# A two-layer transformer kernel: the first feed-forward's residual, and the transposition and absorption of the second layer's weights, as one stage

## Time and profile before

| what | us |
|---|---|
| median of three runs | 3326.28 |
| the profiled execution's own time | 3329.78 |
| its span, first to last instruction | 3328.0 |
| f0r, from its first load | 1346.54 to 1382.10 |
| w1t | 1382.10 to 1425.73 |
| w1u, and the start of w1a | 1425.73 to 1452.12 |
| w1a from its first store | 1452.12 to 1497.60 |
| l1n0 | 1497.60 to 1523.35 |
| l1p0 | 1523.35 to 1601.86 |

### The profile page before, as it was taken

One profiled execution on the slowest core, in us unless ns is written; L12 is line 12 of the kernel. 1 busy time (PEld: TensorE's weight loads), 2 busy tenths in 40 slices (PEclk: granted clock), 3 DMA queues, 4 the chain that ended last, 5 costly groups with the idle time before them and its releaser, 6 DMA issues. The chain is left out here.

```text
span 3328.0 us, 42805 instructions
## 1 busy us (share of the span) xinstructions
PE 2881.2 (87%) x14636; PEld 2302.2 (69%) x14636; DVE 1909.6 (57%) x3654; ACT 1189.4 (36%) x2311; POOL 998.4 (30%) x784
## 2 busy tenths in 40 slices
PE   7969999769999999257799999957999999399994
PEld 6846666547777777237688888746888888288883
DVE  5648877464344444435466666654666666644445
ACT  2226666422222211113244444322444444233331
POOL 1227777534454546303100000033000000222223
PEclk9969999879999999678899999978999999699997
DMA  5764443222111101662000000040000000300002
GB/s 175 232 207 130 133 128 110 68 92 73 46 55 43 57 26 37 217 275 105 28 32 24 23 32 22 18 155 28 23 26 29 22 33 18 125 15 20 19 1 101
DMA packets 137219, 249.58 MB, mean 75 GB/s; under 512 B 14368, under 2 KB 78880, under 8 KB 136320
## 3 DMA queue, kind: packets, MB, share of 16 engines
q1 hardware_dynamic: 137088, 247.91, 22.8%
HBM read 168.43 MB, written 79.17 MB: 74 GB/s over the span
## 5 line engine op out<-in xcount | busy, mean ns | idle before, releaser
L1067 POOL TENSOR_TENSOR l0a_probs_hl<-l0a_probs,l0a_probs_hl 128x896 fp32r<-128x896 f32 (+1 forms) x128 | 284.9, 2245 | 107.1 <-ACT l0a_probs L995 107.1
L1299 PE MATMUL l1a_obank<-l1a_pT_hl,l1k_v_hl 128*128 128x512 f32 (+3 forms) x1152 | 300.7, 370 | 7.2 <-DVE l1a_pT_hl L1372 7.1
L1325 ACT ACTIVATE l1a_probs<-l1a_scores,l1a_row 128x128 f32<-128x128 f32 (+7 forms) x256 | 189.5, 742 | 318.1 <-DVE l1a_row L1362 318.1
L1372 DVE TENSOR_TENSOR l1a_pT_hl<-l1a_work,l1a_pT_hl 128x512 fp32r<-128x512 f32 (+3 forms) x384 | 212.9, 554 | 155.0 <-ACT l1a_pT_hl L1332 154.8
L1415 POOL TENSOR_TENSOR l1a_q_stage<-l1k_qpe,l1a_ones 128x512 fp32r<-128x512 f32 x32 | 33.3, 1041 | 877.0 <-PE l1a_work L1307 820.3
L1279 PE MATMUL l1a_scores<-l1k_kT_hl,l1a_qa_hl 128*128 128x512 f32 (+3 forms) x1152 | 291.9, 362 | 1.5 <-ACT l1a_probs L1325 1.5
L1629 PE MATMUL f0f_ybank<-f0f_wT,f0f_h_hl 128*128 128x512 f32 x768 | 203.5, 417 | 35.4 <-POOL f0f_h_hl L1745 35.3
L1332 ACT CAST l1a_pT_hl<-l1a_work 128x512 fp32r<-128x512 f32 (+3 forms) x384 | 183.7, 478 | 107.6 <-PE l1a_work L1290 106.4
L1307 PE MATMUL l1a_work<-l1a_wov,l1a_oT_hl 128*128 128x512 f32 x768 | 215.2, 403 | 5.0 <-DVE l1a_oT_hl L1391 3.0
L1362 DVE TENSOR_REDUCE l1a_row<-l1a_scores 128x1 f32<-128x128 f32 (+7 forms) x256 | 189.7, 750 | 45.0 <-PE l1a_scores L1282 44.9
L1386 DVE SCALAR_TENSOR_TENSOR l_acc<-l1a_work,l1a_row,l_acc 128x512 f32<-128x512 f32 x256 | 189.4, 750 | 35.5 <-PE l1a_work L1307 27.1
(11 more groups left out here) (253 smaller groups left out, 6202.6 us busy)
## 6 DMA issues: line engine op xcount, KB each, us to landing
v_dram<-l0f_v_rows SPq DMA_DIRECT2D x24, 768.0 KB, 4.2
qk_dram<-l0f_stage SPq DMA_DIRECT2D x128, 128.0 KB, 2.5
l1a_wov<-wov_dram SPq DMA_DIRECT2D x32, 512.0 KB, 3.4
l0a_v_stage<-v_dram SPq DMA_DIRECT2D x32, 384.0 KB, 4.2
l1a_wabs<-wabs_dram SPq DMA_DIRECT2D x32, 384.0 KB, 3.8
l0a_q_stack<-qk_dram SPq DMA_DIRECT2D x32, 256.0 KB, 3.5
l0a_k_stack<-qk_dram SPq DMA_DIRECT2D x32, 256.0 KB, 3.8
f0f_chunk<-in_L_ffn_w_gate_up SPq DMA_DIRECT2D x32, 256.0 KB, 2.8
```

The costliest lines, as they stand in the source:

```text
L1067: nc.gpsimd.tensor_tensor(probs_hl[:, r, 1, 0:wide], probs[:, r, 0:wide], f32(probs_hl[:, r, 0, 0:wide]), ALU.subtract).then_inc(low_done, 1)
L1299: last = pe.matmul(obank[:, c:SPAN], src["v_hl"][:, a, n, :], pT_hl[:, ring(n, s), b, c:SPAN], start=(n == 0 and i == 0), stop=(n == QT * ...
L1325: nc.scalar.activation(probs[s][:, first:first + wide, :].rearrange("p k c -> p (k c)"), scores[:, n % S_AHEAD, 0:wide * P], ACT.Exp, bias ...
L1372: nc.vector.tensor_tensor(pT_hl[:, r, 1, c:SPAN], work[:, slot, c:SPAN], f32(pT_hl[:, r, 0, c:SPAN]), ALU.subtract).then_inc(work_free[slo ...
```

## The change

One function, `residual_and_weights`, replaces the stages f0r, w1t, w1u and w1a; the `clear_semaphores` between f0r and w1t goes.

- VectorE runs the first 6 row steps (LEAD), then alternates: low half of job n, row step 6 + n; then the last row step, then the low halves of the 16 heads. Within a row step bn_aggr is moved behind z of two tiles earlier. ScalarE runs 6 roots, then alternates the copy of job n and root 6 + n. GpSimd adds as before.
- owT shrinks from 16 heads to a ring of 4, filled two heads ahead within the head loop: TensorE turns o_w of head h + 2 before the products of head h, ScalarE copies it (before: VectorE). o_w and q_nope are loaded in four pieces of four heads each, in SyncE's order below.
- wabs and wov get semaphores of their own: ScalarE waits for the store of wabs (h - 2) and of wov (h - 2) separately, SyncE stores wabs as soon as it is ready.
- waT and wpT are allocated outside (right side of the memory, where xT0 was, which is given up at that point) and stay on chip until l1p of batch 0 is over. Their stores to DRAM, for batch 1, move into l1p0, issued by SyncE at its start. l1n0 no longer loads them; l1n1 does.

```diff
-                with phase("f0r") as m:
-                    residual(nc, m, NT, x1, x2, lambda t: acc[:, t, :])
-        clear_semaphores()
-        with phase("w1") as w:
...
+                hold.close()
+                wk = kept.enter_context(phase("wk"))
+                waT = wk.sb("waT", [P, 2, KT, QL + LAT + ROPE], F32R, side="right")
+                wpT = wk.sb("wpT", [P, 2, 3, NH * ROPE], F32R, side="right")
+                with phase("w1") as m:
...
+                    residual_and_weights(nc, m, ident, x1, x2, acc, sources, waT, wpT, wabs_dram, wov_dram)
         clear_semaphores()
...
+def residual_and_weights(nc, m, ident, src, dst, acc, w, waT, wpT, wabs_dram, wov_dram):
+    RING, LAG, HEADS, AHEAD, LEAD = 4, 2, 4, 2, 6
+    ow = m.sb("ow", [P, 2, KT, HEADS * P])
+    owT = m.sb("owT", [P, RING, D])
...
+        @block.sync
+        def _(sp):
+            def load_rows(g):
+                wait(sp, sum_done, QT * (g - 1))
+                sp.dma_start(x[:, g % 2 * QT:(g % 2 + 1) * QT, :],
+                             src[g * SPAN:(g + 1) * SPAN, :].rearrange("(t p) d -> p t d", p=P)).then_inc(x_loaded[g % 2], 16)
+            def store_rows(g):
+                for t in range(g * QT, (g + 1) * QT):
+                    sp.wait_ge(sum_done, t + 1)
+                    sp.dma_start(dst[t * P:(t + 1) * P, :], z[:, t % RING, :]).then_inc(x_stored[t % RING], 16)
+            def load_ow(i):
+                wait(sp, turned, J + HEADS * (i - 1) if i >= 2 else 0)
+                sp.dma_start(ow[:, i % 2], w["ow"][:, :, i * HEADS * P:(i + 1) * HEADS * P]).then_inc(ow_loaded[i], 16)
+            def store_head(h):
+                sp.wait_ge(a_low, h + 1)
+                sp.dma_start(wabs_dram[h], f32(wabs[:, h % 2])).then_inc(a_stored[h % 2], 16)
+                sp.wait_ge(v_low, h + 1)
+                sp.dma_start(wov_dram[h], f32(wov[:, h % 2])).then_inc(v_stored[h % 2], 16)
+            sp.dma_start(qa[:, :, :], w["qa"]).then_inc(down_loaded, 16)
+            sp.dma_start(kva[:, 0, :], w["kva"][0]).then_inc(down_loaded, 16)
+            sp.dma_start(kva[0:ROPE, 1, :], w["kva"][1]).then_inc(down_loaded, 16)
+            load_rows(0)
+            for e in range(2):
+                sp.dma_start(qp[e * ROPE:(e + 1) * ROPE], w["qp"][e]).then_inc(pe_loaded, 16)
+            load_rows(1)
+            load_q(0)
+            load_ow(0)
+            store_rows(0)
+            load_rows(2)
+            sp.dma_start(k_b[:, :, :], w["k_b"]).then_inc(kb_loaded, 16)
+            store_rows(1)
+            load_rows(3)
+            sp.dma_start(v_b[:, :, :], w["v_b"]).then_inc(vb_loaded, 16)
+            load_q(1)
+            load_ow(1)
+            store_rows(2)
+            store_rows(3)
+            load_q(2)
+            for h in range(NH):
+                store_head(h)
+                if h == 1:
+                    load_ow(2)
+                    load_q(3)
+                if h == 5:
+                    load_ow(3)
...
+        @block.tensor
...
+            for h in range(AHEAD):
+                turn(h)
             for h in range(NH):
-                wait(pe, low, 2 * (h - 1))
+                if h + AHEAD < NH:
+                    turn(h + AHEAD)
+                if h % HEADS == 0:
+                    pe.wait_ge(q_loaded[h // HEADS], 16)
+                wait(pe, a_low, h - 1)
                 for j in range(3):
                     last = pe.matmul(abank[:, h % 2, j * P:(j + 1) * P], q_nope[:, h, j * P:(j + 1) * P],
                                      k_b[:, h, :], start=True, stop=True)
+                last.then_inc(a_full, 1)
+                pe.wait_ge(ow_copied, h + 1)
+                wait(pe, v_low, h - 1)
+                pe.matmul(vbank[:, h % 2, :], v_b[:, h, :], owT[:, h % RING, :], start=True, stop=True
+                          ).then_inc(v_full, 1)
         @block.scalar
...
+            for t in range(LEAD):
+                root(t)
+            for n, (blocks, view, hi, lo) in enumerate(jobs):
+                act.wait_ge(turned, n + 1)
+                nc.scalar.copy(hi, view(bank[:, n % RING])).then_inc(job_high, 1)
+                if LEAD + n < NT:
+                    root(LEAD + n)
+            for h in range(AHEAD):
+                copy_ow(h)
             for h in range(NH):
+                act.wait_ge(a_full, h + 1)
+                wait(act, a_stored[h % 2], 16 * (h // 2))
...
+                if h + AHEAD < NH:
+                    copy_ow(h + AHEAD)
+                act.wait_ge(v_full, h + 1)
+                wait(act, v_stored[h % 2], 16 * (h // 2))
...
         @block.vector
+            def row(t):
+                if t < NT:
+                    r = t % RING
+                    nc.vector.bn_stats(stats[:, r, :], acc[:, t, :]).then_inc(stats_done, 1)
+                if t >= LAG:
+                    u = t - LAG
+                    r = u % RING
+                    dve.wait_ge(std_done, u + 1)
+                    nc.vector.reciprocal(rstd[:, r:r + 1], std[:, r:r + 1]).then_inc(rstd_done, 1)
+                    dve.wait_ge(rstd_done, u + 1)
+                    wait(dve, x_stored[r], 16 * (u // RING))
+                    nc.vector.tensor_scalar(z[:, r, :], acc[:, u, :], mv[:, r, 0:1], rstd[:, r:r + 1],
+                                            ALU.subtract, ALU.mult).then_inc(z_done, 1)
+                if t < NT:
+                    r = t % RING
+                    dve.wait_ge(stats_done, t + 1)
+                    nc.vector.bn_aggr(mv[:, r, :], stats[:, r, :]).then_inc(mv_done, 1)
+            for t in range(LEAD):
+                row(t)
+            for n, (blocks, view, hi, lo) in enumerate(jobs):
+                dve.wait_ge(job_high, n + 1)
+                nc.vector.tensor_tensor(lo, view(bank[:, n % RING]), f32(hi), ALU.subtract).then_inc(job_low, 1)
+                if LEAD + n < NT + LAG:
+                    row(LEAD + n)
+            for t in range(LEAD + J, NT + LAG):
+                row(t)
...
-def latent_operands(nc, m, ident, xT_hl, waT, wpT, norm_w, rope, out):
+def latent_operands(nc, m, ident, xT_hl, waT, wpT, norm_w, rope, out, stores=()):
+        @block.sync
+        def _(sp):
+            for dst, tile in stores:
+                sp.dma_start(dst, tile).then_inc(stored, 16)
+            wait(sp, stored, 16 * len(stores))
```

More of the change, by code:

```diff
@@ L1805, in absorbed_weights @@
     wabs = m.sb("wabs", [P, 2, 2, 3, LAT], F32R)
     wov = m.sb("wov", [P, 2, 2, D], F32R)
[L1807 to L1810, removed]
-    with nc.Block() as block:
+    bank = m.ps("bank", [P, RING, SPAN])
+    abank, vbank = m.ps("abank", [P, 2, SPAN]), m.ps("vbank", [P, 2, SPAN])
+    jobs = [([(qa[:, i, c * P:(c + 1) * P], i * P) for i in range(3)] + [(kva[:, 0, c * P:(c + 1) * P], 3 * P)],
+             bank_part(SPAN), waT[:, 0, c, 0:SPAN], waT[:, 1, c, 0:SPAN]) for c in range(KT)]
@@ new lines, in residual_and_weights @@
+    jobs.append(([(kva[0:ROPE, 1, c * P:(c + 1) * P], c * ROPE) for c in range(KT)], bank_part(KT * ROPE, KT),
+                 waT[:, 0, :, SPAN:SPAN + ROPE], waT[:, 1, :, SPAN:SPAN + ROPE]))
+    jobs += [([(qp[:, 4 * g + i, j * P:(j + 1) * P], i * P) for i in range(4)], bank_part(SPAN),
+              wpT[:, 0, j, g * SPAN:(g + 1) * SPAN], wpT[:, 1, j, g * SPAN:(g + 1) * SPAN])
+             for j in range(3) for g in range(2)]
+    J = len(jobs)
+    x_loaded = [m.sem(f"x_loaded{i}") for i in range(2)]
@@ L1835, in _ @@
         @block.vector
         def _(dve):
-            for h in range(NH):
[L1838 to L1845, removed]
-                par = h % 2
-                sp.wait_ge(low, 2 * h + 2)
-                sp.dma_start(wabs_dram[h], f32(wabs[:, par])).then_inc(stored[par], 16)
-                sp.dma_start(wov_dram[h], f32(wov[:, par])).then_inc(stored[par], 16)
-            for par in range(2):
-                sp.wait_ge(stored[par], 32 * NH // 2)
@@ L2168, in two_layers @@
                         with phase(f"l1p{b}") as m:
-                            latent_operands(nc, m, ident, xT, waT, wpT, norm_w, (cos, sin), ops)
+                            latent_operands(nc, m, ident, xT, waT, wpT, norm_w, (cos, sin), ops,
+                                            kept_pairs if b == 0 else [])
+                    kept.close()
                     with phase(f"l1a{b}") as m:
```

151 lines of the change are left out of this document (102 added, 49 removed).

## The result

The changed kernel takes 3284.05 us (median of 4 runs, 3277.77 to 3286.7) against 3326.52 for the kernel before on the same chip: ratio 0.9873, 95% interval 0.9851 to 0.9894, that is 42.5 us less (interval 35 to 50). The prediction said 3285. One execution of e1_keep_only (3652 us) and one of the kernel before (7911 us) were in a slow state of the chip, and the ratios of the experiments leave them out.

What follows compares the result with a forecast made beforehand. DMA engines were taken as the common resource of a serial seam with four kinds of waits. Seam 61.3 + 52 = 113.3 against 151.1 us, 37.8 less, plus 3.3 in the next stage: 41.1 less, median 3285, range 3268 to 3303.

Steps and rivals of the forecast that it cites:

- Steps 1 to 3: Seam from first load through residual rows and weight jobs: first absorbed store at 61.3 us.
- row 0 behind the queued loads: Residual rows: row 0's store moves behind the first queued weight loads, landing at about 25 us, and z(4) waits for it.
- the ring of two engines: Residual rows with jobs: VectorE and ScalarE wait on each other in turn, 3.1 us a row.
- a second queueing at z(12): Residual rows: store 8 lands behind later loads at 51.3 us, so z(12), ready at 49.8, waits.
- Step 4: Head loop: 52 us, the middle between 49.3 (all bytes at 397 GB/s) and 55.4 (no added load absorbed).
- the finer wait: Head loop: ScalarE's first half of a head waits for its own store only, giving back up to 0.2 us a head.
- Step 5: Norm stage of batch 0: without the waT and wpT loads the following stage starts 3.3 us sooner (0 to 4.2).
- Step 6: Batch 0's latent_operands: the moved waT and wpT stores, 5.5 MB taking 32 us, cost nothing there.
- A: Rival for the seam: stores and loads overlap fully and the queue never empties; 3267 us, chance 0.09.
- B: Rival for the head loop: TensorE at 1.2 GHz sets the pace, 63 us instead of 52; 3296 us, chance 0.13.
- C: Rival for the seam: mixed loads and stores drain at 171 GB/s, 15 us more there; 3338 us, chance 0.03.
- D: Rival: a later stage gives the gain back, or rows stay serial behind loads; within 10 us of before, chance 0.05.

Runs made afterwards that it cites:

- e1_keep_only: Kernel before, with waT and wpT kept on chip for batch 0 and their stores moved into latent_operands: seam 143.3 us, ratio to before 0.9963.
- e4: Changed kernel with eight buffers instead of four for the normalised rows z: seam 105.4 us, ratio to before 0.9860.
- e5: Changed kernel with the first four heads' q_nope and o_w loads issued behind the first four row stores: seam 115.6 us, ratio to before 0.9870.
- e3: Changed kernel with bn_aggr directly behind bn_stats, ahead of reciprocal and z: seam 113.1 us, ratio to before 0.9879.
- e8: Changed kernel without the q_nope and o_w loads for heads 8 to 15 (wrong operands): head loop 41.5 us, ratio to before 0.9847.
- e9: Changed kernel with each head's three query-side products computed three times: head loop 54.7 us, ratio to before 0.9888.
- e2: Changed kernel with waT and wpT stored in the seam and read back in batch 0's norm stage: seam 128.1 us, ratio to before 0.9934.
- e10: Changed kernel with seven z buffers, earlier bn_aggr, qp on even/odd partitions, three absorbed-operand buffers, later last q_nope load: seam 98.0 us, ratio to before 0.9853.
- e7: Changed kernel with eight z buffers and qp's halves loaded into even and odd partitions: seam 99.2 us, ratio to before 0.9825.

## Why the prediction was right

**Steps 1 to 3, the rows part.** Forecast 61.3, measured 62.5, with errors that cancel. The first row's store was issued 12.5 us after the first load, not 10.5, and z(4) came at 27.2, not 25. Against that the turn of a row is 2.86 us, not 3.1: from the start of the statistics to that of the aggregate, with reciprocal and z between, it takes 1.24 us, where 0.72 + 0.71 = 1.43 were summed. z(12) came at 53.0 after a wait of 3.5, where 51.3 and 1.5 were forecast. The mechanisms (row 0 behind the queued loads, the ring of two engines, a second queueing at z(12)) are confirmed by e4 and e5, by e3, and by e4 in turn. The wait of k_b's issue, 10.69 us in the earlier trace rows, was rightly not charged: its issue takes 2.48 us here.

**Step 4, the head loop.** Forecast 52, measured 53.3. The sum was right by luck: its two terms were 45.5 for the loop and 6.5 for the late loads, and they measure 41.5 and 11.7 (e8). The picture of even heads near 3 us apart was wrong too: a head takes 2.2 to 2.3 us between the loads, with waits of 5 to 6 us behind each bunch of them. The loads are not half absorbed but paid for in full, while the loop itself became 4.0 us shorter, of which the prediction had the finer wait at up to 0.2 us a head. The rate of 397 was about right (392 for the stores alone). Transposes and copies at nothing: e9 bears it out.

**Step 5, the norm stage.** Forecast 3.3 less, measured 2.3 in the changed kernel, and 3.1 to 4.1 in the other kernels that keep the operands (only e2 doesn't: 1.0). The mechanism holds: the DMA share is 0.39, SyncE's wait no longer ends the stage, and the next stage starts 0.5 us after the last arithmetic, as against 4.2 before. The missing 1 us is at the other end: the first rows arrive 6.7 us after the stage's first load, where it was 5.6.

**Step 6, the moved stores.** Nothing was charged and nothing shows: 77.0 us against 78.5, a difference within what this stage shows over all kernels (77.0 to 79.9).

**The sum.** Seam and norm stage give 35.3 + 2.3 = 37.6 where I had 41.1. The median fell by 42.5, with an interval of 35 to 50 in which 37.6 lies too. Between them lie 3.6 us in the latent stage of batch 1, which the prediction did not have, and about 1 us that can't be told from variation. The closeness of 3284 to 3285 is therefore in part luck: the steps named give about 3.5 us less than forecast, and a clock effect that was not forecast gives as much more.

**The rivals.** A (3267) needed a queue that never empties; it is what e10 approaches, with other buffers, and not this change. B: the clock of the head loop did fall, to 0.82, after waits, but TensorE is not the bound (e9). C: where the DMA share is near 1 the lowest rate is 207 GB/s, and only for qp, whose cause is its partitions (e7), not the mix of loads and stores; lower rates, 121 and 122 GB/s, go with shares of 0.45 and 0.33, a queue short of work. D: nothing was given back in a later stage.

**Left open.** Why the last products of batch 1's latent stage keep the full clock. In both kernels with the old order of stages (before and e1) this stretch of two stages takes 104.4 to 104.6 us, in all eleven with the merged one 100.7 to 101.0. So it goes with the merge, not with the kept operands, although the same products stand there. No run here changes only the start of that stage, so what shifts the clock is not shown.

## What to carry to other kernels

When a serial seam is merged so that loads and ring stores share one queue, count the bytes issued ahead of each store that a ring waits for; here four buffers more for 8 KB of SBUF per partition took 10 us off the seam, and moving the loads behind the stores nothing. In the merged seam the bytes that were added or left out cost what the queue needs for them (5.5 MB 12 us, 3.67 MB 11.7 us), so a store that was partly hidden before (5.5 MB at 8 us in the seam) is worth more to remove. Look at GB/s beside the DMA share: here a share near 1 at 210 GB/s came from a load into 64 neighbouring partitions, and the same bytes went at 377 GB/s into every second partition.

## What the hardware showed that I had not expected

- A load into 64 neighbouring partitions moves 207 to 217 GB/s, the same load into every second partition 377, both at a DMA share of 1.06 to 1.10.
- A head's two stores (0.92 MB) drain in 2.2 to 2.3 us; a window of 14 us with such stores alone has 392 GB/s, close to the fastest row.
- Equal work in an unchanged stage ran at a granted clock of 1.00 in one kernel and 0.66 and 0.83 in the other, 3.6 us apart. The stretch takes the longer time in both kernels with the old order of stages and the shorter in all eleven with the merged one.
